# Adding the bias of dt on VectorE instead of ScalarE in a fused Mamba and feed-forward layer, with one more wait on GpSimd

## The reference

```python
xz = einsum('bld,ed->ble', x, W_in);  xi, z = split(xz, 2)
u  = silu(causal_conv(xi, conv_w, 4 taps) + conv_b)
dbl = einsum('blc,ec->ble', u, W_xproj)             # 16 for dt, 16 for B, 16 for C
dt = softplus(einsum('blr,cr->blc', dbl[..., :16], W_dt) + b_dt)
h  = h * exp(dt * A) + (dt * u) * B                 # scan over time, A = -exp(A_log)
y  = (sum_s h * C + u * D_skip) * silu(z)
x1 = layernorm(x + y @ W_out.T)
out = layernorm(x1 + (silu(x1 @ w_gate.T) * (x1 @ w_up.T)) @ w_down.T)
```

## Time and profile before

| | us |
|---|---|
| three runs, median | 1802.52 |
| three runs, lowest and highest | 1801.61, 1809.47 |
| the profiled execution | 1808.44 |
| its span, first to last instruction | 1806.7 |
| busy in the span: PE, ACT, DVE, POOL | 1738.0, 1712.5, 1683.7, 1482.0 |

### The profile page before, as it was taken

The page is one execution under the profiler, slowest core; times in us unless marked ns, Lnnn a source line. Parts: engine busy times, 40 slices in busy tenths (PEclk is TensorE's granted clock), DMA queues, the critical chain, the costliest instruction groups (busy, mean ns, idle before and its releaser), DMA issues.

```text
span 1806.7 us, 40364 instructions
## 1 busy us (share of the span) xinstructions
PE 1738.0 (96%) x15678; PEld 1216.0 (67%) x15678; DVE 1683.7 (93%) x1970; ACT 1712.5 (95%) x2907; POOL 1482.0 (82%) x852
## 2 busy tenths in 40 slices
PE   7778999999999999999999999999999999999997
PEld 3455676766767676676767767676676767667676
DVE  5999999999999999999999999999999999999974
ACT  6898999999999999999999999999999999999971
POOL 5896897979979798997979979797997979889850
PEclk9899999999999999999999999999999999999999
DMA  7040130303113040131303013040221304022000
GB/s 210 1 120 1 4 118 15 118 1 86 47 16 117 13 120 2 18 115 15 118 2 103 29 15 118 14 119 1 47 86 15 118 1 126 7 38 83 1 24 24
DMA packets 171487, 100.57 MB, mean 56 GB/s; under 512 B 139408, under 2 KB 157584, under 8 KB 163232
## 3 DMA queue, kind: packets, MB, share of 16 engines
q1 hardware_dynamic: 171296, 97.98, 18.8%
HBM read 88.52 MB, written 9.44 MB: 54 GB/s over the span
## 4 chain that ended last, share of the span: by engine, by line
PE 41%; ACT 24%; DVE 11%; issue 11%; POOL 11%; SPq 0%; DMA 0%; ACTq 0%; POOLq 0%; DVEq 0%
PE ring L1160 14%; PE tp L1139 11%; POOL drive L568 9%; ACT decay L704 8%; ACT hT L711 7%; DVE h L915 7%; PE yb L1153 6%; PE ring L1252 4%; DVE acc L936 2%; PE ring L1228 2%; PE ring L1197 1%; ACT acc L720 1%; ACT L741 1%; ACT yt L732 1%; POOL diag_c L576 1%
## 5 line engine op out<-in xcount | busy, mean ns | idle before, releaser
L568 POOL TENSOR_TENSOR drive<-dtu,b_all 128x1024 f32<-128x1024 f32 x511 | 1208.4, 2396 | 8.6 <-DVE h L915 5.7
L704 ACT ACTIVATE decay<-dt,a_neg 128x512 f32<-128x512 f32 x1024 | 705.4, 718 | 15.7 <-DVE h L915 14.9
L915 DVE TENSOR_TENSOR_SCAN h<-decay,h,drive 128x512 f32<-128x512 f32 x512 | 620.2, 1267 | 9.6 <-ACT decay L704 6.5
L1139 PEld LDWEIGHTS tp<-ident,h 128*128 128x128 f32 x4096 | 463.4, 141 | 238.2 <-issue 124.0
L915 DVE TENSOR_TENSOR_SCAN h<-decay,drive 128x512 f32<-128x512 f32 x512 | 592.3, 1209 | 28.6 <-ACT decay L704 25.7
L711 ACT ACTIVATE hT<-tp 128x512 f32<-128x512 f32 x1024 | 595.5, 618 | 13.3 <-PE tp L1139 12.3
L1139 PE MATMUL tp<-ident,h 128*128 128x128 f32 x4096 | 563.2, 277 | 36.3 <-ACT hT L711 28.0
L1153 PE MATMUL yb<-hT,diag_c 128*32 128x128 f32 x8192 | 275.7, 277 | 7.1 <-ACT yt L732 5.2
L1153 PEld LDWEIGHTS yb<-hT,diag_c 128*32 128x32 f32 x8192 | 210.8, 110 | 82.7 <-issue 48.2
L1160 PE MATMUL ring<-xt,w_in 128*128 128x512 f32 x512 | 245.1, 602 | 2.3 <-ACT acc L752 2.3
L936 DVE SCALAR_TENSOR_TENSOR acc<-xi,cw,acc 128x512 f32<-128x512 f32 x189 | 163.9, 888 | 14.5 <-ACT xi L722 10.6
(11 more groups left out here) (132 smaller groups left out, 1647.8 us busy)
## 6 DMA issues: line engine op xcount, KB each, us to landing
b_all<-bc_scratch SPq DMA_DIRECT2D x63, 1024.0 KB, 6.8
xt<-in_xT SPq DMA_DIRECT2D x16, 512.0 KB, 4.3
res<-in_x SPq DMA_DIRECT2D x16, 512.0 KB, 6.2
out<-res SPq DMA_DIRECT2D x15, 512.0 KB, 2.9
c_col<-bc_scratch SPq DMA_DIRECT2D x256, 2.0 KB, 2.4
bc_scratch<-dbl SPq DMA_DIRECT2D x16, 64.0 KB, 1.6
b_all<-bc_scratch SPq DMA_DIRECT2D x2, 512.0 KB, 4.5
w_g<-in_w_gT SPq DMA_DIRECT2D x1, 768.0 KB, 7.1
```

The costliest lines, as they stand in the source:

```text
L568: tt(drive[:, j % 4, :, :], src, b_all[:, n:n + 2, :], ALU.mult).then_inc(g_dr, 1)
L704: act(decay[decay_slot(k.parity, i)][:, :], dt[:, cb, :], ACT.Exp, scale=a_neg[:, cb, n:n + 1]).then_inc(a_da, 1)
L915: nc.vector.tensor_tensor_scan(h[:, h_slot(k.parity, q), at:at + T, i % 4], decay[decay_slot(k.parity, i)][:, :], drive[:, (i // 2) % 4, i ...
L1139: last = nc.tensor.transpose(tp[g % 2][:, b * P:(b + 1) * P], h[:, h_slot(k.parity, q), t0:t0 + TS, :].rearrange("p t s -> p (t s)"), iden ...
```

## The change

For chunks 1 to 15 the addition of the dt bias moves from ScalarE to VectorE, as a `tensor_scalar` (L963 in the new numbering) that reads the ring bank and writes `acc`. In the steady tables it stands at (9, 3), (13, 0), (15, 1) and (15, 3), in the first table at (9, 1), (10, 2), (12, 1) and (14, 2). Only the four additions for chunk 0 itself, ahead of the loop, stay on ScalarE (`first_bias`). The semaphore is renamed from `a_xb` to `dt_raw` and is now raised by VectorE; it is what ScalarE's exp and TensorE's next product in that bank wait for. Beside this GpSimd gets an entry `("yield", 0)` at (4, 0) of the steady table, behind drive unit 8: it waits there until the first convolution step of the chunk ahead is done on VectorE.

```diff
 ACT_SIDE:
-    (9, 3): [("hT", 35), ("bias", 0)]       +    (9, 3): [("hT", 35)]
-    (13, 0): [("bias", 1), ("y", 2)]        +    (13, 0): [("y", 2)]
-    (15, 1): [..., ("bias", 2), ...], (15, 3): [("bias", 3)]
 DVE_SIDE:
+    (9, 3): [("bias", 0)],
+    (13, 0): [("bias", 1)],
+    (15, 1): [("bias", 2)],
+    (15, 3): [("bias", 3)],
 POOL_SIDE:
-    (3, 1): [("std", 1)], (4, 1): [("diag", 2)],
+    (3, 1): [("std", 1)], (4, 0): [("yield", 0)], (4, 1): [("diag", 2)],
...
+                if what == "yield" and head:
+                    wait(eng, v_conv, conv_steps(k + 1, 1))
...
-            def add_bias(k, cb):
+            def first_bias(k, cb):
                 wait(eng, p_dt, k.count(4, cb + 1))
-                act(acc[:, cb, :], bank(k, "dt", cb)[:, :], ACT.Identity, bias=bdt[:, cb:cb + 1]).then_inc(a_xb, 1)
+                act(acc[:, cb, :], bank(k, "dt", cb)[:, :], ACT.Identity, bias=bdt[:, cb:cb + 1]).then_inc(dt_raw, 1)
...
-                wait(eng, a_xb, k.count(4, 2 * half + 2))
+                wait(eng, dt_raw, k.count(4, 2 * half + 2))
...
+            def add_bias(k, cb):
+
+                wait(eng, p_dt, k.count(4, cb + 1))
+                ts(acc[:, cb, :], bank(k, "dt", cb)[:, :], bdt[:, cb:cb + 1], None, ALU.add).then_inc(dt_raw, 1)
...
-                    "dt": (a_xb, k.count(4, n + 1)),
+                    "dt": (dt_raw, k.count(4, n + 1)),
```

More of the change, by code:

```diff
@@ L75 @@
     (8, 2): [("hT", 30)], (8, 3): [("hT", 31)], (9, 0): [("hT", 32), ("hT", 33), ("tanh", 4)],
[1 row of a table removed]
[1 row of a table added]
     (10, 1): [("hT", 37), ("tanh", 5), ("y", 1), ("hT", 38), ("hT", 39)], (10, 3): [("hT", 40)],
     (11, 0): [("hT", 41)], (11, 1): [("hT", 42), ("hT", 43)], (11, 3): [("sz", 2)],
[1 row of a table removed]
[1 row of a table added]
     (13, 2): [("hT", 48)], (13, 3): [("sz", 3), ("hT", 49), ("log", 0)], (14, 2): [("hT", 50), ("hT", 51)],
[2 rows of a table removed]
[2 rows of a table added]
 }
 DVE_SIDE = {
-    (2, 1): [("skip", 3)], (3, 3): [("conv", 0, 0), ("r1", 0)], (4, 2): [("r1", 1)],
+    (2, 1): [("skip", 3)],
+    (3, 3): [("conv", 0, 0), ("r1", 0)],
+    (4, 2): [("r1", 1)],
     (5, 3): [("max", 1), ("norm", 0), ("conv", 0, 1), ("conv", 1, 0), ("conv", 1, 1), ("conv", 2, 0), ("conv", 2, 1), ("conv", 3, 0), ("conv", 3, 1)],
[L87 to L90, removed]
+    (6, 0): [("gs", 0), ("gs", 1)],
+    (6, 2): [("hid", 0)],
+    (7, 0): [("gs", 2)],
+    (7, 1): [("hid", 1)],
+    (8, 2): [("gs", 3), ("skip", 0)],
+    (9, 2): [("gs", 4)],
+    (9, 3): [("bias", 0)],
+    (10, 3): [("hid", 2), ("gs", 5)],
+    (11, 3): [("hid", 3), ("hid", 4)],
+    (12, 1): [("skip", 1)],
+    (12, 2): [("hid", 5)],
+    (13, 0): [("bias", 1)],
+    (14, 0): [("r2", 0), ("skip", 2)],
+    (14, 1): [("max", 0)],
+    (15, 0): [("r2", 1)],
+    (15, 1): [("bias", 2)],
+    (15, 3): [("bias", 3)],
 }
 POOL_SIDE = {
-    (3, 0): [("gate", 3), ("diag", 1)], (3, 1): [("std", 1)], (4, 1): [("diag", 2)], (5, 0): [("diag", 3)],
+    (3, 0): [("gate", 3), ("diag", 1)], (3, 1): [("std", 1)], (4, 0): [("yield", 0)], (4, 1): [("diag", 2)], (5, 0): [("diag", 3)],
     (5, 1): [("std", 0)], (6, 0): [("heads", 0)], (7, 1): [("dtu", 1)], (12, 1): [("gate", 0)],
@@ L124 @@
 DVE_FIRST = {
-    (2, 2): [("max", 1)], (3, 2): [("conv", 0, 0)],
+    (2, 2): [("max", 1)],
+    (3, 2): [("conv", 0, 0)],
     (7, 0): [("conv", 0, 1), ("conv", 1, 0), ("conv", 1, 1), ("conv", 2, 0), ("conv", 2, 1), ("conv", 3, 0), ("conv", 3, 1)],
-    (10, 0): [("skip", 0)], (12, 3): [("skip", 1)], (13, 3): [("max", 0)],
-    (14, 2): [("skip", 2)],
+    (9, 1): [("bias", 0)],
+    (10, 0): [("skip", 0)],
+    (10, 2): [("bias", 1)],
+    (12, 1): [("bias", 2)],
+    (12, 3): [("skip", 1)],
+    (13, 3): [("max", 0)],
+    (14, 2): [("skip", 2), ("bias", 3)],
 }
@@ L416, in mamba_ffn @@
         a_da = sem("a_da"); a_ev = sem("a_ev"); a_xi = sem("a_xi"); a_u = sem("a_u"); a_z = sem("a_z")
-        a_sz = sem("a_sz"); a_xb = sem("a_xb"); a_dbl = sem("a_dbl"); a_e = sem("a_e"); a_ln = sem("a_ln")
+        a_sz = sem("a_sz"); dt_raw = sem("dt_raw"); a_dbl = sem("a_dbl"); a_e = sem("a_e"); a_ln = sem("a_ln")
         a_y = sem("a_y"); a_x1T = sem("a_x1T"); a_th = sem("a_th"); a_o = sem("a_o"); a_set = sem("a_set")
@@ L796, in item @@
                     copy_dbl(k + 1)
-                if what == "bias" and head:
-                    add_bias(k + 1, i)
                 if what == "log" and i == 0 and head:
@@ L846, in _ @@
             act(a_neg[:, :, :], a_neg[:, :, :], ACT.Exp).then_inc(a_set, 1)
-            add_bias(k0, 0)
-            add_bias(k0, 1)
+            first_bias(k0, 0)
+            first_bias(k0, 1)
             for cb, (e, ln) in enumerate(((f_e, f_ln), (a_e, a_ln))):
-                eng.wait_ge(a_xb, cb + 1)
+                eng.wait_ge(dt_raw, cb + 1)
                 act(dt[:, cb, :], acc[:, cb, :], ACT.Exp).then_inc(e, 1)
@@ L855, in _ @@
             decay_step(k0, 0, True)
-            add_bias(k0, 2)
+            first_bias(k0, 2)
             decay_step(k0, 1, True)
-            add_bias(k0, 3)
+            first_bias(k0, 3)
             for half in range(2):
@@ L993, in item @@
                 i, *part = of or [None]
+                if what == "bias" and head:
+                    add_bias(k + 1, i)
                 if what == "max":
```

## The result

The changed kernel takes 1820.00 us in the median of five runs (1818.51 to 1820.42). The kernel before, run beside it, takes 1803.87 (1801.61 to 1809.47, five runs). The ratio over the runs made side by side is 1.0072, with a 95% interval of 1.005 to 1.0094 (the two medians alone give 1.0089): slower, by more than the half per cent that the prediction took as its bound. The forecast was 1805, with a range to 1815; the time lies above it. The profiled execution took 1820.42, its span 1818.6, against 1808.44 and 1806.7 before.

What follows compares the result with a forecast made beforehand. No single engine was taken as the bound (TensorE 96%, ScalarE 95%, VectorE 93% busy). Profiled: 1808.44 - 8.7 + 7 = 1806.7 us; for the median, 1805 was taken between 1800.8 and 1809.5, range 1792 to 1815.

Steps and rivals of the forecast that it cites:

- Step 1: First convolution step of chunk 1: with GpSimd waiting it runs at once, and the chunk gets 8.7 us shorter.
- The rival that the wait gives next to nothing: Chunk 1: a blocked step loses one turn only, so under 2.2 us is gained; profiled time 1813.2, chance 0.05.
- Step 2: Wait on GpSimd in chunks 2 to 14: costed at nothing; 2.6 us in all if the room were gone.
- Steps 3 and 4: Chunks 0 to 14, four additions each: ScalarE loses 2.3 us a chunk, VectorE gains 2.5, with no new wait for TensorE.
- Step 5: Steady chunks: VectorE's added 2.5 us lengthen odd chunks by 0.9 and even by 0.2; 7 us over 14 chunks.
- of which I count 0.8 in the even chunk: TensorE's waits for ScalarE, 1.0 us a chunk: 0.8 won back in even chunks, nothing in odd ones.
- The waits ahead of scan 3: Odd chunk's end into the next: VectorE's waits of 0.76 and 0.36 us cover 1.1 of the additions' 2.5.
- the 1.1 us for down in the even chunk: VectorE's waits for the product down: they stay in even chunks, as VectorE is not late there.
- Step 6: Chunk 0: 2.3 us off ScalarE against 2.5 on VectorE, so no change, 1 us either way.
- The second: VectorE is the bound, at the last three and first four scans: 1.2 us a chunk, median about 1815, chance 0.22.
- a distance over 109 us: Between first convolution steps of successive chunks: over 109 us would mean VectorE was the bound; forecast was 108.0 to 108.8.
- The first rival: ScalarE is the bound: steady chunks shorten by at most half a us each, -7 us, median about 1791, chance 0.23.

Runs made afterwards that it cites:

- wait_only: The kernel before with the wait on GpSimd added and no addition moved: 1799.78 us median, ratio 0.9952.
- bias_only: The changed kernel without the wait on GpSimd, so only the additions moved to VectorE: 1822.19 us median, ratio 1.0081.
- narrow_add: The changed kernel with the additions on VectorE made over 8 of 512 columns, the rest left out: 1795.73 us median, ratio 0.9932.

## Why the prediction was wrong, point by point

**Step 1, the wait in chunk 1: -8.7 forecast.** Chunk 1 came down by 7.6, and the missing 1.1 are its additions. In wait_only it is 107.87 long, 8.7 less than 116.56. The mechanism was right. The rival that the wait gives next to nothing falls with it. The Trainium skill ("SBUF — State Buffer", section "Who interferes with whom") says that a VectorE instruction with two SBUF inputs and a GpSimd instruction that reads SBUF block each other for a whole instruction. The exclusion is there, but one turn is not all that the step can lose: it lasted 9.3 us in two profiles, 2.7 in bias_only, where it did lose one turn, and 0.7 where GpSimd stands still.

**Step 2, the wait elsewhere: nothing.** Right; 107.63 and 108.03 with it, 107.58 and 107.97 without. The 0.2 us for the handover were 0.1 in chunk 1 (158.59 to 158.67).

**Steps 3 and 4, the prices of the addition: 2.3 us a chunk from ScalarE, 2.5 on VectorE.** Right on VectorE, which has 2.41 more in an even and 2.39 in an odd chunk than in wait_only; one addition is 726 ns, 1 ns from the row that the text went by. On ScalarE the instructions are gone, but its busy time fell by only 1.18 and 1.77 us (107.25 and 107.02 in wait_only, 106.07 and 105.25 after), where the text expected it at 104.5. Why isn't shown; in narrow_add it fell by 1.66 and 1.90. That there is no new wait for TensorE held in the steady chunks: the 1.6 us of the group are those of chunk 0.

**Step 5, what the 2.5 us do: here it failed.** Forecast were 0.9 in the odd and 0.2 in the even chunk; measured against wait_only, 1.18 and 1.15. The failing step reads "of which I count 0.8 in the even chunk": that TensorE would get back its waits for ScalarE, there and not in the odd chunk. Here are TensorE's waits in chunk 8 of the kernel before, and then of the kernel after:

```profile
PE yb L1153 <- ACT yt L732: 0.4, 1, 0.4
PE tp L1139 <- ACT hT L711: 0.3, 1, 0.3
```

```profile
PE tp L1167 <- DVE h L936: 0.8, 2, 0.5
PE yb L1181 <- ACT yt L755: 0.4, 1, 0.4
PE tp L1167 <- ACT hT L734: 0.3, 1, 0.3
```

The even chunk never had 0.8 us of these waits: the 1.0 was the mean of 0.7 in even and 1.3 to 1.4 in odd chunks. Both waits stay to a tenth, and a new one of 0.8, for VectorE, comes on top. Where a wait for ScalarE can be won back, it is in the odd chunk. These are chunk 9 of wait_only, then of narrow_add, then of the changed kernel:

```profile
PE tp L1141 <- ACT hT L713: 1.0, 2, 0.6
```

```profile
PE tp L1167 <- ACT hT L734: 0.3, 1, 0.3
```

```profile
PE tp L1167 <- ACT hT L734: 1.2, 2, 0.8
```

With little work on VectorE 0.7 us of the wait go, and with the whole additions they are back. The 1.0 us a chunk was put down to ScalarE as the engine that is late, and so taken as a gain once ScalarE has less to do. But in the kernel after ScalarE itself waits. Its waits over the 13 chunks:

```profile
ACT decay L727 <- DVE h L936: 23.8, 26, 1.5
ACT hT L734 <- PE tp L1167: 15.1, 40, 1.6
```

Its decays wait for scans to free a bank (4.3 us outside the stall before), and its copies of states wait for the transposes (2.1 before), which wait for scans. The work came off an engine that was itself held in step with VectorE.

The other term of step 5, what VectorE's work costs before any relief, was too small as well. Forecast were 1.0 us in the even chunk and 0.9 in the odd one for all of the 2.5; from narrow_add to the changed kernel 2.1 us of that work alone cost 1.39 and 1.61. The relief was at least 0.24 in the even chunk, for 0.8 forecast, and at least 0.43 in the odd one, for nothing forecast. So that the odd chunk came within 0.3 us is partly luck: two errors cancel in it. With no work at all on VectorE the relief was not measured, so the exact split between the two terms stays open. (The 0.3 us "of small waits" in the odd chunk's sum has no row behind it either.)

Two more sentences of step 5 were off. The waits ahead of scan 3 were taken as room for all of the odd chunk's additions; yet VectorE still waits for decays after the change, 11.0 us in 13 chunks where it was 21.1. And the 1.1 us for down in the even chunk were to stay, but in chunk 8 they fell to 0.4. VectorE did take 1.1 to 1.2 us a chunk out of its idle time; the other half of its new work made the chunk longer. A wait that stands in a loop (scan for decay, decay for a bank that an earlier scan frees) is only part room; that is how we read these rows, and no run takes the loop apart.

**Step 6, chunk 0: nothing, 1 us either way.** Too small: +3.7 in the profile, +2.9 in the mean of several, in a chunk that differs by up to 4 us between profiles of the same instructions. The text set 2.3 us against 2.5 and did not ask whether the product was there at the new place, as it had for the steady chunks. At one it came 1.6 us too late.

**The median.** The forecast halved the stall, between 1800.8 and 1809.5. The median of the five runs beside the changed kernel is 1803.87, so the change could take little from it. That was the luck of five runs. Of the 69 made beside the experiments 41 are in the upper group; the medians of the three sets are 1809.11, 1808.96 and 1808.33, and against those the changed kernel would be 11 to 12 us slower, not 16. By the experiments the medians add up: wait_only at 1799.8, 14 chunks by 1.16 are 16.3, and chunk 0 by medians 1.9, together 1818.0 against 1820.0; in the profiles the changed kernel also starts 1.0 us later than wait_only, and its end is 1.3 longer.

**The rivals.** The second, VectorE as the bound, had the size: 1.2 us a chunk, 17 us. Its reason was that nothing but the waits ahead of scan 3 covers the work and that ScalarE's relief brings nothing. The relief did bring something, 0.24 and 0.43 us at least, and the work cost more before it, so that the size is in part luck. Its place was not right either: the late and the early additions cost about alike. Its time of 1815 was held down by the same guess on the median, and lacked chunk 0. Of the text's own signs for it, a distance over 109 us, the odd chunks have one (109.2) and the even ones don't (108.8). The first rival, ScalarE as the bound, falls: the steady chunks got longer, and even with most of the new work away, in narrow_add, the relief brings 0.3 us a chunk in the mean.

## What to carry to other kernels

When several engines are over 93% busy in lockstep, read for each wait on the engine to be relieved who holds that engine up in turn; a wait for ScalarE is no gain to be had if ScalarE itself waits for the engine that gets the work. Moving 2.3 us of work between two such engines cost half of it here, with no hinge seen: an engine's idle time need not be room where it is part of a loop, and each new place of a moved instruction has to be checked for its operand, in the first chunk too. And look at the two halves of a change apart: here the one-line wait alone gives 0.5%, and the other half took more than that away.

## What the runs showed of the hardware that was not expected

A VectorE instruction with two SBUF inputs that meets GpSimd's products lost many turns in a row, but not always: the same convolution step lasted 9.32 and 9.34 us in two profiles of one kernel and 2.72 in bias_only, each time issued 0.2 us behind the start of the same GpSimd instruction; it lasted 1.5 to 1.8 in the steady chunks of all kernels, and 0.72 where GpSimd stood still. A `tensor_scalar` from a bank to SBUF takes 201 ns for 8 columns, 459 for 256 and 726 for 512, so about 1.04 ns a column and 0.2 us at the least. And with identical instructions chunk 0 was up to 4 us apart (99.0 to 103.2), at a granted clock of TensorE of 0.79 or 0.51 in one stretch of 8 us.
